# Reordered first loads, an even three maxima per step, and lambda's chain moved into attention

## What is computed

```python
# attention: 16 sub-heads of 8 features, in pairs (8 heads), values of 16 features
q, k = rope(xn @ Wq.T) / sqrt(8), rope_inv(xn @ Wk.T)
probs = softmax(q @ k.T)                       # all 1024 keys, no mask
lam = exp(sum(lambda_q1 * lambda_k1)) - exp(sum(lambda_q2 * lambda_k2)) + LAMBDA_INIT
attn = (probs[pair 0] - lam * probs[pair 1]) @ v
attn = attn * rsqrt(mean(attn**2) + 1e-5) * (1 - LAMBDA_INIT)
# zones: a router on the mean of xn picks 3 of 8 feed-forward nets for each sequence
h = tanh(mean(xn) @ W1 + b1); w = top3(softmax(h @ W2 + b2)), normalised
zones = sum over the 3 picked e of w[e] * gelu(xn @ Wa[e]) @ Wb[e]
return x + attn @ Wo.T + zones
```

## Time and profile before

| | us |
|---|---|
| median of three runs (lowest, highest) | 429.36 (429.24, 430.72) |
| the profiled execution | 429.37 |
| its span | 427.6 |
| PE busy | 412.2 |
| DVE busy | 383.8 |
| ACT busy | 344.1 |
| POOL busy | 146.1 |

### The profile page before, as it was taken

How to read it: one execution, slowest core, us unless ns; L and a number is a source line. 1 busy time by engine, 2 the same in 40 slices (tenths; PEclk the granted TensorE clock), 3 DMA queues, 4 the chain that set the end, 5 groups by cost and what they waited for, 6 DMA issues and landing times.

```text
span 427.6 us, 7728 instructions
## 1 busy us (share of the span) xinstructions
PE 412.2 (96%) x2750; PEld 191.0 (45%) x2750; DVE 383.8 (90%) x737; ACT 344.1 (80%) x459; POOL 146.1 (34%) x179
## 2 busy tenths in 40 slices
PE   8998999999999999999999999999999999999996
PEld 6664566566665333333333333333333333335544
DVE  4989999999999899999999999999999999888575
ACT  2787765675654799889899989989999999989993
POOL 4159998988863500111020110120103303420000
PEclk9999999999999999999999999999999999999999
DMA  9726760400000060020002054000000000000003
GB/s 268 304 92 208 264 231 22 138 13 1 3 0 2 16 233 2 4 98 4 2 1 101 1 129 71 3 2 2 3 2 2 3 0 3 2 3 2 2 2 100
DMA packets 21872, 24.95 MB, mean 58 GB/s; under 512 B 11818, under 2 KB 16106, under 8 KB 21578
## 3 DMA queue, kind: packets, MB, share of 16 engines
q1 hardware_dynamic: 21096, 23.60, 17.5%
q10 hardware_dynamic: 738, 0.86, 0.8%
HBM read 14.49 MB, written 8.65 MB: 54 GB/s over the span
## 4 chain that ended last, share of the span: by engine, by line
PE 74%; DVE 11%; ACT 7%; issue 5%; DMA 1%; POOL 1%; ACTq 0%
PE ps L1395 21%; PE ps L1358 16%; PE ps L1248 13%; ACT E L809 6%; DVE part_max L924 6%; PE ps L1320 4%; PE ps L1173 3%; PE ps L1175 3%; PE ps L1174 3%; PE ps L1386 3%; PE ps L1321 2%; PE ps L1322 2%; PE ps L1376 2%; DMA X<-in_x 1%; PE ps L1350 1%
## 5 line engine op out<-in xcount | busy, mean ns | idle before, releaser
L924 DVE TENSOR_REDUCE part_max<-ps 128x1 f32<-128x512 f32 x512 | 320.6, 681 | 21.9 <-PE ps L1248 15.0
L809 ACT ACTIVATE E<-ps 128x1024 f32<-128x1024 f32 x256 | 245.3, 1029 | 29.3 <-PE ps L1358 25.9
L1395 PE MATMUL ps<-E,Vg 128*32 128x512 f32 x896 | 119.3, 604 | 0.0
L1248 PE MATMUL ps<-K,Q 32*128 32x512 f32 x384 | 104.2, 463 | 1.4 <-DVE part_max L924 1.1
L1358 PE MATMUL ps<-Q,K 32*128 32x512 f32 x320 | 70.8, 489 | 2.1 <-ACT E L809 1.4
L559 POOL TENSOR_TENSOR hL<-h,hH 128x512 fp32r<-128x512 f32 x48 | 61.4, 1288 | 13.1 <-ACT hH L769 11.2
L1358 PEld LDWEIGHTS ps<-Q,K 32*128 32x128 f32 x320 | 28.6, 181 | 82.7 <-ACT E L809 72.3
L767 ACT ACTIVATE h<-ps 128x512 f32<-128x512 f32 x48 | 28.8, 601 | 33.6 <-PE ps L1175 25.1
L1248 PEld LDWEIGHTS ps<-K,Q 32*128 32x128 f32 x384 | 44.4, 182 | 23.9 <-DVE part_max L924 19.3
L610 POOL TENSOR_TENSOR U<-AT,rsum 128x256 f32<-128x256 f32 x15 | 9.3, 623 | 102.4 <-DVE rsum L1060 102.4
L1248 PE MATMUL ps<-xnL,xnH 32*128 32x512 f32 x128 | 41.8, 454 | 0.9 <-DVE part_max L924 0.7
(11 more groups left out here) (171 smaller groups left out, 418.0 us busy)
## 6 DMA issues: line engine op xcount, KB each, us to landing
K<-k_scr SPq DMA_DIRECT2D x5, 512.0 KB, 3.8
Q<-q_scr SPq DMA_DIRECT2D x5, 512.0 KB, 7.1
tab<-in_tables SPq DMA_DIRECT2D x2, 1024.0 KB, 10.0
wa_raw<-in_wa SPq DMA_DIRECT2D x6, 256.0 KB, 2.9
wb_raw<-in_wb SPq DMA_DIRECT2D x6, 256.0 KB, 3.2
Q<-max_turned SPq DMA_DIRECT2D x80, 2.0 KB
X<-in_x SPq DMA_DIRECT2D x2, 512.0 KB, 7.0
k_scr<-V SPq DMA_DIRECT2D x2, 512.0 KB, 10.9
```

Of the source, the lines that this page charges most:

```text
L809: nc.scalar.activation(E[:, par, 2 * jj:2 * jj + 2, :].rearrange("p j t -> p (j t)"), ps[:, 2 * jj:2 * jj + 2, :].rearrange("p j t -> p (j ...
L924: nc.vector.tensor_reduce(part_max[:, tile // FC % 2, j * FC + tile % FC, sh:sh + 1], ps[:, SLOT_BANK[x], :], AX.X, ALU.max).then_inc(slot ...
L1248: mm(ps[:, SLOT_BANK[x], :], Qs[g % KQ_BUFS][strip(j), tile % TB * P:(tile % TB + 1) * P], Ks[g % KQ_BUFS][strip(j), sh * BANK:(sh + 1) * ...
L1395: last = mm(ps[QUAD * j:QUAD * (j + 1), B_PV, :], Vg[:, par, st, j // 2, :], E[:, s % 2, k, :], start=(st == 0), stop=(st == TB - 1), skip ...
```

## The change

The first loads: SP issues X of batch 0, then `w_in` and `cst` (which ACT issued before), then X of batch 1, then the tables. ACT issues the six small tensors first and `strips` behind them. The slots: `max_slots` gives four slots in step 0 and three in each step from 1 to 120; nothing else about them is changed. Lambda's chain is cut into four parts of three instructions, which DVE runs in steps 13, 29, 45 and 61, behind the slots of that step.

```diff
-MAX_STEPS, PACE_STEPS = 121, 98
+MAX_STEPS = 121
 def max_slots(s):
-    own = GJ * 2 * TB
     def up_to(n):
-        if n <= PACE_STEPS:
-            return GJ * LEAD - (-n * (GJ * (QUADS - LEAD) - own) // PACE_STEPS)
-        return GJ * QUADS - own + min(own, -(-(n - PACE_STEPS) * own // (MAX_STEPS - PACE_STEPS)))
+        return min(GJ * LEAD + (3 * n + 1 if n else 0), GJ * QUADS)
     return [divmod(x, 4) for x in range(up_to(s), up_to(s + 1))]
+LAMBDA_AT = (13, 29, 45, 61)
...
         def _(sp):
-            for b in range(BATCH):
+            def x_load(b):
                 sp.dma_start(X[:, b * TB:(b + 1) * TB, :], ...).then_inc(x_in[b], 16)
+            x_load(0)
+            sp.dma_start(w_in[:], wqkv).then_inc(w_arr, 16)
+            sp.dma_start(cst[:], consts).then_inc(c_in, 16)
+            x_load(1)
             for kind in range(2):
                 sp.dma_start(tab[:, 2 * kind:2 * kind + 2, :], ...).then_inc(tab_in[kind], 16)
...
         def _(act):
-            act.dma_start(cst[:], consts).then_inc(c_in, 16)
-            act.dma_start(w_in[:], wqkv).then_inc(w_arr, 16)
-            act.dma_start(h[0:QUAD, 0, :], strips).then_inc(sel_in, 16)
             for dst, src in ((w1_in, w1), ..., (lam_in, lam), (wo_in, wo)):
                 act.dma_start(dst[:], src).then_inc(s_in, 16)
+            act.dma_start(h[0:QUAD, 0, :], strips).then_inc(sel_in, 16)
...
-            lambdas()
             for n in range(UNITS):
                 for t, k in lead_slots(n):
                     reduce_slot(t, k)
...
+            def lambdas(part):   # the same twelve instructions, three to a part
...
             for s in range(ALL_STEPS):
                 for t, k in max_slots(s):
                     reduce_slot(t, k)
...
                     query_rows(s // TB - 1, (s // TB - 1) % 2, s % TB)
+                if s in LAMBDA_AT:
+                    lambdas(LAMBDA_AT.index(s))
                 if s in SUMS_AT:
                     sums_turn(SUMS_AT.index(s))
```

More of the change, by code:

```diff
@@ L1048, in _ @@
                     rotary(EARLY // 2, (n - (UNITS - 2),))
+            def lambdas(part):
+                nl, ab, cc, c2, nlc = (lt[:, k:k + 1] for k in range(5))
+                if part == 0:
+                    dve.wait_ge(lam_exp, 1)
+                    link(nc.vector.scalar_tensor_tensor(nl, lam_e[:, 1:2], LAMBDA_INIT, lam_e[:, 0:1],
+                                                        ALU.subtract, ALU.subtract))
+                    link(nc.vector.tensor_scalar(ab, nl, -1.0, None, ALU.mult))
+                    link(nc.vector.tensor_tensor(ab, ab, nl, ALU.max))
+                elif part == 1:
+                    link(nc.vector.tensor_scalar(ab, ab, 1.0, None, ALU.add))
+                    link(nc.vector.reciprocal(cc, ab))
+                    link(nc.vector.tensor_scalar(cc, cc, LAMBDA_RANGE, 1.0, ALU.mult, ALU.min))
+                elif part == 2:
+                    link(nc.vector.tensor_tensor(c2, cc, cc, ALU.mult))
+                    link(nc.vector.tensor_scalar(epsc[:], c2, EPS, SQRT_LEAST, ALU.mult, ALU.max))
+                    link(nc.vector.tensor_scalar(limit[:], c2, FLT_MAX, None, ALU.mult))
+                else:
+                    link(nc.vector.tensor_tensor(nlc, nl, cc, ALU.mult))
+                    link(nc.vector.tensor_scalar(comb[:], cst[:, C_E0:C_E0 + 2 * QUAD], cc, None, ALU.mult))
+                    nc.vector.scalar_tensor_tensor(comb[:], cst[:, C_E1:C_E1 + 2 * QUAD], nlc, comb[:],
+                                                   ALU.mult, ALU.add).then_inc(comb_done, 1)
             def query_rows(a, th, part):
```

## The result

The changed kernel takes 436.18 us (median of four runs, 435.09 to 438.01), the kernel before 430.04 beside it: the ratio is 1.0137, with an interval of 1.011 to 1.0165. The change makes the kernel slower by 1.1 to 1.7%, where the prediction said 429.1 and "same". The profiled execution of the changed kernel has the median's time, 436.18; its span is 434.4, 6.8 more than before's 427.6. I account for these 6.8 us; the medians differ by 6.1.

A forecast was written before the change was run, and what follows sets the result against it. PE was taken to set the pace, with POOL beside it in the zones and DVE in four-slot steps. Terms -0.2 - 1.05 + 1.1 - 3.0 + 0.75 + 2.1 = -0.3 gave 429.1 us from 429.37; range 427.0 to 431.2.

The forecast's parts named there:

- same: Whole kernel: a time between 427.2 and 431.5 us, not told from no change; chance 0.75.
- loads: At the start: X of batch 0 lands earlier, of which PE gets back at most 0.22 us; -0.2 us.
- lambda out of the zones' start: Zones' start: unit 1's second product 1.77 us earlier, of which POOL's packed work lets 1.08 fit; -1.05 us.
- lambda into attention: Steps 13, 29, 45, 61: 2.4 us of DVE work, priced by the sums' transpose's ratio; +1.1 us.
- fourth slots less: Attention steps 16, 32, 49, 65, 81: five fourth slots fewer, which had made DVE the bound; -3.0 us.
- third slots late: Attention steps 102, 107, 111, 116, 120: five third slots more, costing little where two stood; +0.75 us.
- half 13's wait: Before step 104's scores: the turn of half 13 comes 3.2 us later against 1.06 of slack; +2.1 us.
- a rival: Start: `strips`, behind six small loads, lands late and delays ACT's root; 429.5 to 433.3 us, chance 0.14.
- The 0.22 of idle before the transposes: Start: PE's idle between warm-up's end at 11.58 and the transposes at 11.81, taken as the most the loads could gain.

The follow-up runs named there:

- e11: The changed kernel with 40 warm-up matmuls on PE in place of 30: 434.95 us, ratio 1.0117.
- e4: The changed kernel with eight throwaway matmuls on PE before its wait for half 13's rows: 434.82 us, ratio 1.0082.
- e9: The changed kernel with `wo_in` issued behind `strips` (five small loads, `strips`, `wo_in`): 432.41 us, one execution.
- e8: The changed kernel with `strips` issued first on ACT's queue, half 13 turned behind slot 448 and lambda's chain back in front of the zones: 428.56 us, ratio 0.9943.
- e7: The kernel before with only the new `max_slots` and half 13 turned behind slot 448: 429.29 us, ratio 0.9959.
- e10: The changed kernel with ACT's table load and first activation ahead of its DMAs, then `strips`, then the six small loads: 433.47 us, one execution.
- e1: The changed kernel with `strips` issued first on ACT's queue, ahead of the six small tensors: 432.67 us, ratio 1.0046.
- e2: The changed kernel with half 13 turned behind slot 448 in place of slot 451: 432.52 us, ratio 1.0034.
- e5: The kernel before with only the change's new order of loads, `strips` last in ACT's queue: 433.15 us, ratio 1.006.
- e3: The changed kernel with `strips` issued first on ACT's queue and half 13 turned behind slot 448: 429.17 us, ratio 0.9962.

## Why the prediction was wrong

Terms as predicted, and as the profiled changed kernel and the runs size them:

```
term                              predicted   measured   from
loads                               -0.2       +2.64     2.17 strips, 0.47 clock (e11)
lambda out of the zones' start      -1.05      -0.89     u0 to u8
half clock at the zones' end          -        +1.12     u45 to s1; cause open
lambda into attention               +1.1       +1.14     four windows, 68.73 - 67.59
fourth slots less                   -3.0       -2.44     five windows, 84.89 - 87.33
third slots late                    +0.75      +0.98     0.29 to s113, 0.76 after, -0.07 before s103
half 13's wait                      +2.1       +2.15     e4's 2.44 less 0.29
half clock behind it                  -        +2.12     4.56 less e4's 2.44
sum                                 -0.3       +6.82
```

**The loads: the step that failed.** The prediction priced `strips` rightly, as a rival ("a landing past about 8.4 begins to cost, one for one"), and then gave it 0.14 because the small loads "are now the first of their queue, three issues earlier". They were, and it did not help: `strips` landed with 10.7, the root came 2.2 late, and 2.17 were lost, with 0.47 of half clock behind them. The rows of the two queues between 3.4 and 10.7 us of the changed kernel (packets, MB, share of the time of 16 engines) show why:

```profile
q1 hardware_dynamic: 1729, 2.23, 96.8%
q10 hardware_dynamic: 306, 0.13, 6.9%
```

In 7.3 us ACT's queue moved 0.13 MB, about what `wo_in` and `strips` hold, beside 2.23 MB of SP's. Rows 8 had shown the same queue at this pace (154 packets in 3.3 us, 47 per us; here 306 in 7.3, 42 per us; in e9's rows 34 and 42); that was the number to go by, in packets: the bytes of these four rows differ far more (0.00 to 0.04 MB per us). The prediction set against it the Trainium skill's rule that a DMA engine takes turns between queues ("DMA: Bandwidth & Descriptors", "Queues, rings and completion order"). In these rows the small queue had 306 of 2035 packets, 15%; turns of one recorded packet each, as I had read the rule, they were not. The 0.22 of idle before the transposes was no bound for the gain either: the warm-up ended at 10.39 in e8, where it ended at 11.58 before, and unit 0 came 0.64 earlier. That it ended early looks like the execution's luck and not the loads' doing: with the old loads it ended at 10.62 in e7, with `strips` first at 11.59 in e10. In e7 PE then waited for XN until 11.77. e8's transposes, at 11.18, are 0.59 ahead of that, which the new order with `strips` first can give where the warm-up lets it.

**The clock: a term that was missing.** The prediction let a PE wait cost its own length. Behind half 13 it cost 2.15 and then 2.12 more, and at the start 0.47 more. All nine PE idles over 2 us in the profiles after the change (two in the changed kernel; one each in e1, e2, e4, e5, e9, e10, e11) have a half clock that begins during them or within 1.2 us of their end; where e4 and e11 filled the idle with work, it was gone there. A forecast with a wait of 2.1 us in it needed a price for the clock behind that wait; the trace of before, at full clock throughout, has no row for one.

The Trainium skill ("TensorE: Matmul & The Clock Gate", "What's actually happening") says that the clock falls to 1.2 GHz when PE idles; the two levels (granted clock 0.50 to 0.51, and 1.00) and the fall after the idles of 2.15 to 3.24 us agree. A half clock at the zones' end stands in four profiles here (the changed kernel, e3, e10, and a little later e1) and one that begins near 30 us in two (e4, e7), without such an idle before them. I changed nothing that would settle their cause, so it stays open. But the +1.12 need not belong to the change: 40 of the 53 other executions of the kernel before had less than the full clock too, and spans 0.3 to 3.4 us longer than the fast quarter (where in them the half clock lies, no trace shows). Both the forecast and this account start from an execution of before without such a stretch; that is one reason why the profiles differ by 6.8 and the medians by 6.1.

**Right by mechanism and size.** Half 13: the turn came 4.91 later than before in absolute time, 3.41 in the kernel's own pace (step 103 was 1.50 late), where 3.2 were worked out; PE's idle was 2.16 for 2.1, and the wait cost 2.15. That this was avoidable is e2. Lambda out of the zones: 1.75 at unit 1 for 1.77, of which 0.86 was taken back by unit 8, with POOL busy for 21.62 of the 21.70 us from 44.30 on. Lambda into attention: 1.14 for 1.1, from the ratio of the sums' transpose; its DVE work was of the size assumed, 0.15 for most of the instructions, and so was the two-input one, which had been held by POOL before:

```profile
L1040 DVE TENSOR_TENSOR lt<-lt 128x1 f32<-128x1 f32 x1 | 0.2, 160 | 0.0
```

**Right by mechanism, off in size.** The five windows gave 2.44 of the 3.0; alone, in e7, 2.69. The late third slots, with whatever else the last steps lost, cost 0.98 and not 0.75: 0.20 each, so they are not the near-free slots that one window with step 102 had suggested.

## What to carry to other kernels

A load on which the chain of waits hangs belongs in front of its queue, however small the loads ahead of it look: price it by the packets that the queue moved, in the trace, beside the large transfers of the other, not by its place alone. Where an edit creates a PE wait of 2 us, add a price for the clock behind it, or give PE something to do while it waits. When work is evened out over steps, look for the one consumer that now gets its data last: moving half 13's turn by three slots took the changed kernel from a ratio of 1.0137 to 1.0034 (e2). And read the granted clock of several executions before one of them is taken as the base: here it was of the fast quarter.

## What was unexpected in the hardware

A wait of 2.16 us cost 4.3 at the end of its stretch, because the 6.9 us behind it ran at 0.51 of the clock; where that stretch was 3.4 long (e1), steps 103 to 113 lost 3.58 and not 4.56.

What a stretch of half clock costs depends on what PE does in it: 3.4 us of it cost 0.47 at the start, 1.1 at the zones' end and 1.6 near 30 us (e7, from the transposes to unit 0); 6.9 us of it behind half 13 cost 2.1. And such stretches come in places where PE had hardly idled (e3 at 133.40), in some executions and not in others with the same work there.

A DMA issue of ACT's queue that stands behind a table load in program order went out during it (e10: issued at 0.86, the load ran from 0.72 for 1.28).
